# Split of the last phase's down product from chunk 3 instead of 5, and another cut of its first routing

## The reference, cut to what matters

```python
def _L3_ffn_ref(hidden_states, gate_w, gate_bias, w_gate, w_up, w_down, sh_gate, sh_up, sh_down):
    h = hidden_states.reshape(-1, Hd)
    scores = jax.nn.sigmoid(h @ gate_w.T)                    # 32 experts
    sc = scores + gate_bias
    group_scores = jax.lax.top_k(sc.reshape(-1, 8, 4), 2)[0].sum(-1)
    gmask = one_hot(top_k(group_scores, 4)).sum(1)           # 4 of 8 groups
    masked = jnp.where(repeat(gmask, 4) > 0, sc, 0)
    tki = jax.lax.top_k(masked, 8)[1]
    tkw = scores[tki]; tkw = tkw / (tkw.sum(-1) + 1e-20) * 2.5
    combine = (one_hot(tki, 32) * tkw[..., None]).sum(1)
    g = silu(einsum('th,eih->tei', h, w_gate)); u = einsum('th,eih->tei', h, w_up)
    routed = einsum('tei,ehi->th', g * u * combine[:, :, None], w_down)
    shared = silu(h @ sh_gate.T) * (h @ sh_up.T) @ sh_down.T
    return routed + shared
```

## Time and profile before

| | us |
|---|---|
| median of 3 runs | 830.77 |
| lowest, highest | 827.47, 830.89 |
| the profiled execution, its own time | 830.12 |
| its span, first to last instruction | 828.3 |

### The profile page before, as it was taken

One profiled execution on the slowest core, in us unless ns is written; L12 is line 12 of the kernel. 1 busy time (PEld: TensorE's weight loads), 2 busy tenths in 40 slices (PEclk: granted clock), 3 DMA queues, 4 the chain that ended last, 5 costly groups with the idle time before them and its releaser, 6 DMA issues.

```text
span 828.3 us, 13555 instructions
## 1 busy us (share of the span) xinstructions
PE 803.4 (97%) x4387; PEld 558.5 (67%) x4407; DVE 497.6 (60%) x1419; ACT 439.6 (53%) x801; POOL 450.3 (54%) x432
## 2 busy tenths in 40 slices
PE   4999999999999999999999999999999999999998
PEld 4876677676767666665666666656665576677776
DVE  6766536385755637235555767676766647486744
ACT  1434564555646343323667767666566654546543
POOL 5274646557663536467455453454546357575463
PEclk9799999999999999999999999999999999999999
DMA  8213030233414333341233222223122142415151
GB/s 315 81 60 98 6 103 1 64 102 121 144 51 128 77 117 88 114 141 39 64 103 88 79 69 73 72 70 77 36 68 72 33 144 66 152 53 168 56 182 59
DMA packets 44871, 75.29 MB, mean 91 GB/s; under 512 B 8993, under 2 KB 9633, under 8 KB 44673
## 3 DMA queue, kind: packets, MB, share of 16 engines
q1 hardware_dynamic: 44656, 74.42, 30.1%
q10 hardware_dynamic: 144, 0.01, 0.0%
HBM read 56.11 MB, written 1.51 MB: 70 GB/s over the span
## 4 chain that ended last, share of the span: by engine, by line
PE 88%; DVE 7%; ACT 2%; issue 2%; DMA 1%; SPq 0%; DVEq 0%; ACTq 0%
PE Y L979 17%; PE B L892 11%; PE B L894 11%; PE B L893 11%; PE B L1641 5%; PE B L1622 4%; PE B L1660 4%; PE B L1628 3%; PE T L1440 2%; DVE mxh L1931 2%; PE B L1621 1%; PE Y L971 1%; PE Y L970 1%; PE Y L969 1%; PE T L996 1%
## 5 line engine op out<-in xcount | busy, mean ns | idle before, releaser
L1276 POOL TENSOR_TENSOR shared<-shared,bcs 128x512 f32<-128x512 f32 x192 | 247.7, 1296 | 202.7 <-DVE shared L1336 148.9
L1130 ACT ACTIVATE shared<-B 128x512 f32<-128x512 f32 x204 | 121.9, 599 | 206.4 <-PE B L894 205.5
L1336 DVE TENSOR_TENSOR shared<-shared,B 128x512 f32<-128x512 f32 x168 | 114.9, 686 | 172.2 <-PE B L894 132.6
L979 PE MATMUL Y<-shared,down_lo 128*128 128x512 f32 x336 | 172.0, 595 | 0.0
L1870 POOL TENSOR_TENSOR shared_r<-shared_r,const 128x512 fp32r<-128x512 f32 (+1 forms) x128 | 115.7, 936 | 74.3 <-PE B L1622 44.1
L1931 DVE TENSOR_REDUCE mxh<-B 128x4 fp32r<-128x512 f32 (+1 forms) x128 | 78.8, 618 | 81.0 <-PE B L1622 80.0
L1796 ACT ACTIVATE shared<-B 128x512 f32<-128x512 f32 (+1 forms) x128 | 69.5, 543 | 62.5 <-PE B L1628 61.3
L1807 ACT COPY shared<-B 128x512 f32<-128x512 f32 (+1 forms) x128 | 64.5, 504 | 24.8 <-PE B L1641 24.7
L892 PE MATMUL B<-shared_r,gate_hi 128*128 128x512 f32 x102 | 75.0, 736 | 0.0
L1641 PE MATMUL B<-const,shared 128*128 128x128 f32 x448 | 71.5, 276 | 0.7 <-ACT shared L1807 0.7
L892 PE MATMUL B<-x_lo_r,gate_hi 128*128 128x512 f32 x102 | 70.9, 695 | 0.0
(11 more groups left out here) (328 smaller groups left out, 1528.7 us busy)
## 6 DMA issues: line engine op xcount, KB each, us to landing
bcs<-wrow SPq DMA_DIRECT2D x96, 256.0 KB, 3.6
shared_r<-shared_r SPq DMA_DIRECT2D x256, 64.0 KB, 2.0
bcs<-wrow SPq DMA_DIRECT2D x128, 128.0 KB, 3.0
gate_lo<-in_moe SPq DMA_DIRECT2D x9, 256.0 KB, 5.3
up_lo<-in_moe SPq DMA_DIRECT2D x9, 256.0 KB, 6.1
down_lo<-in_moe SPq DMA_DIRECT2D x9, 256.0 KB, 3.7
small<-in_small SPq DMA_DIRECT2D x1, 1372.5 KB, 11.3
X<-in_x SPq DMA_DIRECT2D x4, 256.0 KB, 5.4
```

Source lines behind the costliest of these rows:

```text
L979: nc.tensor.matmul(Y[:], w_raw[2][:, at:at + P], hid[(n0 + c) % HIDDEN], start=(i == 0), stop=(i == m["NC"] - 1))\
L1130: nc.scalar.activation(sg[(n0 + n) % ACTIVE], B[n % GATES][:], ACT.Silu).then_inc(sem("sg_ready"), 1)
L1276: gp.tensor_tensor(by_weight, by_weight, bcs[(PLACE.k0[p] + r // m["PER"]) % BROADCAST], ALU.mult)\
L1336: nc.vector.tensor_tensor(hid[(n0 + n) % HIDDEN], sg[(n0 + n) % ACTIVE], up[:], ALU.mult)\
```

## The change

The routing of phase 7's group 0 is cut in other places: a `yield` behind the reciprocal makes two pieces of the first, and the one behind the groups' mask (`gm`) is left out, so that the mask and the masked scores are one piece. WHOLE goes from 5 to 3: chunks 3 and 4 of groups 1 to 3 are split as well. The high and low parts of the down weights' piece 0 (chunks 3 and 4) are made too, at steps 9 (ScalarE) and 14 (GpSimd); piece 1 moves from step 9 to 10 on ScalarE. `down_hi` takes 14 chunks of columns instead of 12, so `hid_hi` starts one tile higher.

```diff
-        WHOLE, HIGHS = 5, 10
+        WHOLE, HIGHS = 3, 10
...
-        hid_hi = [late.at_tile(18 + i, [P, TG], shared_r) for i in range(HIGHS)]
+        hid_hi = [late.at_tile(19 + i, [P, TG], shared_r) for i in range(HIGHS)]
...
-            return slice((a - WHOLE) * P, (b - WHOLE) * P)
+            return slice((max(a, WHOLE) - WHOLE) * P, (b - WHOLE) * P)
+
+        def down_raw(q):
+
+            a, b = PIECES[7][q]
+            return slice(max(a, WHOLE) * P, b * P)
...
                 st.add(v.reciprocal(t["sig"][:], t["sig"][:]))
                 st.settle()
+                yield
...
             st.add(v.tensor_scalar(t["gm"][:], t["gwork"][:, :, 0:NGR], TAKEN, None, ALU.is_equal))
             st.settle()
-            yield
+            if (p, g) != (7, 0):
+                yield
...
-                    if (g, i) == (1, a):
-                        pe.wait_ge(sem("down_lo_ready"), q)
+                    if (g, i) == (1, max(a, WHOLE)):
+                        pe.wait_ge(sem("down_lo_ready"), q + 1)
...
-        DOWN_ACT = {9: 1, 11: 2, 13: 3}
-        DOWN_POOL = {18: 1, 22: 2, 26: 3}
+        DOWN_ACT = {9: 0, 10: 1, 11: 2, 13: 3}
+        DOWN_POOL = {14: 0, 18: 1, 22: 2, 26: 3}
```

More of the change, by code:

```diff
@@ L1137, in stream_act @@
                     act.wait_ge(sem(f"raw1_{q}"), 96)
-                    nc.scalar.copy(down_hi[:, down_piece(q)], w_raw[2][:, piece(7, q)])\
+                    nc.scalar.copy(down_hi[:, down_piece(q)], w_raw[2][:, down_raw(q)])\
                         .then_inc(sem("down_hi_ready"), 1)
@@ L1280, in stream_pool @@
                     q = DOWN_POOL[n]
-                    c = piece(7, q)
-                    pool.wait_ge(sem("down_hi_ready"), q)
+                    c = down_raw(q)
+                    pool.wait_ge(sem("down_hi_ready"), q + 1)
                     after_down(pool, 7, 0, PIECES[7][q][1] - 1)
```

## The result

The changed kernel takes 832.11 us as the median of 12 runs (829.21 to 833.18); the kernel before, run beside it on the same chip, 829.64 us (12 runs, 827.30 to 830.89). The ratio is 1.0036 with a 95% interval of [1.0025, 1.0046], so the change costs about 3.0 us [2.1, 3.8]; the two medians lie 2.5 us apart. That lies within the 0.5% that the prediction calls the same, and the time lies in its range. But a change of nothing lies outside the interval, and so does the forecast of +0.6 us: the cost is about five times as large.

The account below looks back on a forecast made before the run. TensorE, busy nearly all the time, was taken as the bound. Attention -0.26, group 2's wait +1.5 and later split products -0.64 gave +0.6 us; 830.7 profiled or 831.4 by median, forecast 831.0 us, range 827.7 to 833.2.

Parts of the forecast that it names:

- Part 4: Phase 7, group 2: late weights delay silu 6, so chunk 8's gate product waits, 1.5 us later; group 3 costs nothing.
- bounds of nothing and 2.0 us: Limits on TensorE's shift at group 2's wait: nothing if weights land earlier, 2.0 us if each hop takes 0.1 more.
- Part 1: Attention: cutting the routing's first piece moves unit 6's shift from 649.93 to 648.7; 0.94 us gain after unit 7.
- signs of being wrong: No TensorE idle in group 2, idle in group 1 or 3, or a span moved by more than 3 us.
- rival of a second wait: Group 2's backlog makes TensorE wait for a low part once more, up to 2.0 us: 832.7 us; chance 0.15.
- last rival: Attention stall reappears a unit later, group 1 banks come at VectorE's pace; 830.1 to 830.8 us; chance 0.08.
- Part 3: Phase 7: six down products change from whole to split, 0.16 us each, 0.96 us less TensorE work.
- Part 2: Attention: merged mask and masked scores meet GpSimd, taking back 0.68 us, leaving 0.26; doubted that the pairs would wait.

Follow-up runs that it names:

- e3: Changed kernel with the old routing cuts and chunks 3 and 4 split in group 3 only; 828.77 us, 0.9995 of the kernel before.
- e4: Changed kernel with ScalarE's copy of the turned weights one step earlier, ahead of the cast of chunk 14; 828.76 us, 0.9999 of the kernel before.
- e6: Kernel before with the new routing cuts, GpSimd's last key copy held until VectorE's maximum of unit 7; 828.03 us, 0.9985 of the kernel before.
- e8: e7 with the down product split from chunk 1 on (WHOLE = 1); 827.50 us, 0.9986 of the kernel before.
- e2: Changed kernel with the old routing cuts, so the split from chunk 3 alone; 831.40 us, 1.0030 of the kernel before.
- e7: Changed kernel with the earlier weights copy of e4 and the held key copy of e6; 827.35 us, 0.9977 of the kernel before.
- e1: Kernel before with the new routing cuts alone, split still from chunk 5; 829.69 us, 1.0012 of the kernel before.
- e5: Kernel before with the earlier weights copy of e4, split from chunk 5, old routing cuts; 829.42 us, 0.9999 of the kernel before.

## Why the prediction was right and wrong

**Right: the wait of group 2.** Part 4 named the place, the chain and the order, and each link is in the trace. GpSimd started chunk 3 a little earlier than the chain had it (product at 754.53 + 0.89 = 755.42 in before's time, forecast 755.7), so the table load came 2.47 us later than in the earlier trace rows instead of 2.7. The gate product came 1.22 us later and the one behind it 1.57, where I had 1.5; the idle time itself was 1.17 us, below the 1.5 to 1.8 that I had named. The bounds of nothing and 2.0 us hold both.

**Right: the form of the result.** 42 split down products stand in the trace, six more than before. The unit-6 idle is gone, its shift coming at 647.65 + 1.05 = 648.70 as Part 1 had it, and the kernel is slower by less than 0.5%. The new wait stands at unit 7, but with 1.25 us, where I had some tenths. And one of my own signs of being wrong came: idle time in group 3.

**Wrong: "In group 3 no sigmoid follows, the weighing of chunk 4 at 792.39 waited only for the product, and all of it has 2 us of room. I cost both at nothing."** This is the step that failed, and the largest. The rows told how chunk 4 stood with the weights landing when they did before. But that landing is set by ScalarE's copy at the end of group 2, and Part 4 itself made ScalarE 2.7 us late in group 2. The copy came 3.2 us later against the phase, chunk 3 was weighed 0.9 us late for the DMA alone, and group 3 lost 0.73 us at the wait of 0.47 and 1.08 at the wait of 0.81. At the down product of 795.80, ahead of both waits, TensorE was 0.34 + 0.89 = 1.23 us late against the phase's start, and behind them, at the transposes of group 2's result, 2.19 + 0.89 = 3.08 us: 1.85 us more, in a group where I had counted a gain. I followed the backlog to the next wait and stopped. e3 (no wait in group 3 without group 2's backlog) and e4 (no wait anywhere once the weights land early) show the way it took.

**The rival of a second wait had the size and not the mechanism.** It asked for 2 us through VectorE's backlog and the four upper banks in group 2, with the routing's pieces hitting GpSimd. One such hit is in the trace (1.26 us at 772.88), and it made the backlog longer; but no upper bank was waited for in group 2. The second wait came one group later through the weights. My argument against it, that "the backlog shrinks with every chunk", set the chain's pace (1.95 us a chunk) against TensorE's (2.10). The copy, though, hangs on the chain, and the chain was as late at chunk 10 as at chunk 6 (2.46 us).

**The last rival was half right.** It said that the attention's stall would reappear a unit later through sum and pairs: it did. It also said that TensorE would be handed its banks at VectorE's pace in group 1: what Part 3 saves there is partly lost for this reason, as told below. It didn't have the waits of groups 2 and 3.

**Wrong: Part 2's doubt about the pairs.** I took 0.26 us of gain for the attention and gave 0.8 us of loss as the bound if sum and pairs had to wait for GpSimd's four operations. The attention lost 0.16 us. The pairs rose from 0.52 to 1.70 us beside the key copy and are 0.53 in e6, where the copy is held back. The Trainium skill (SBUF — State Buffer, "Who interferes with whom") says that a VectorE instruction with two SBUF inputs contends with a GpSimd one that reads SBUF, and that the one that issues later is blocked for the whole instruction. The trace agrees: the three pairs took 1.70 us beside GpSimd operations of 0.58 us each, and the masked scores 1.30 us beside one of 1.26 us. That the pairs were short in the earlier trace rows said nothing, because nothing ran on GpSimd beside them there. The loss stayed below the bound because the sum (0.28 us) slipped in ahead. The mask hardly waited (0.23 us at 652.48, 0.18 in phase 7), and the masked scores did (1.30 us, 0.70 in phase 7), but no shift waited for them: with unit 7 already late, TensorE came later.

**Part 3's saving is there, though not all of it.** Once the waits are gone, e4's phase 7 is 0.69 us shorter than before where six times 0.16 is 0.96; in e3 two chunks gave 0.18 of 0.32, in e8 six more gave 0.43 of 0.96. Read against before, e4's TensorE gains 0.30 us at the two chunks of group 1, 0.31 in group 2 and 0.29 in group 3, close to 0.32 each. It loses 0.13 us again late in group 1, most of it at one upper product that starts right behind a low part of VectorE. TensorE and VectorE, e4:

```profile
738.07 0.48 PE L899 MATMUL B<-shared_r,up_hi 128*128 128x512 f32 x1
```

```profile
737.31 0.69 DVE L1324 TENSOR_TENSOR shared_r<-B,shared_r 128x512 fp32r<-128x512 f32 x1
```

The low part ends at 738.00. Before, 0.27 us lay between its end and the upper product, so TensorE can hardly get further ahead there than that. In e8 the wait of 0.16 us stands at the same place. Another 0.08 us goes near the end of group 3, in e3 too; where it goes stays open.

**The sum, put right**: attention +0.16 us (forecast -0.26); behind group 2's wait +1.57 (+1.5); the two split chunks of group 2 -0.34 (-0.32); group 3's two waits +1.85 (nothing); the split chunks of group 3 -0.29 (-0.32). That is 2.95 us, where I had +0.6. The waits of group 3 make 1.85 us of the miss of 2.35, the attention 0.42.

## What to carry to other kernels

When a change makes an engine late, follow the lateness past the first wait: to whatever that engine hands over at the end of the group (here the copy that starts the next group's DMA), and ask what now depends on its landing. A form of work that is cheaper on the busiest engine but needs its input earlier is worth its saving only where that input is early; moving one copy on another engine turned +2.8 us into -0.7 us in that phase. Before a short VectorE operation is moved, look at what GpSimd does at the new place: there, three pairs went from 0.52 to 1.70 us and one of 128 x 4 numbers from 0.17 to 1.26.

## What the runs showed of the hardware

**A 128 x 4 operation can take 1.26 us.** The `tot` row above writes and reads four numbers per partition. It began 0.05 us behind a GpSimd operation of 1.29 us and ended with it. e2, e4, e7 and e8 have the same coincidence and 1.26 to 1.28 us; where the operation falls between two weighings, in before, e1, e3, e5 and e6, it takes 0.17 us. So in these rows the time is set by the neighbour on GpSimd and not by the operation's own size.

**The clock dips behind an idle time in some executions only.** TensorE works at its full clock of 2.4 GHz in this stretch before. The profiled execution of e1 shows, a few microseconds behind the idle time of 1.24 us, a stretch at the lower level of 1.2 GHz (windows: stretch, us, busy time of PE, PEld, DVE, ACT, POOL, granted clock, DMA share, GB/s; a window that holds both levels shows their mean):

```profile
656.00:660.00 4.00, 4.00 (x27) 1.85 (x25) 2.05 (x15) 2.00 (x4) 0.05 (x1) 0.73 0.00 0
```

and e4, where the same work stands:

```profile
656.00:660.00 4.00, 3.91 (x21) 2.45 (x21) 1.12 (x4) 1.40 (x5) 0.00 (x0) 0.62 0.00 0
```

e3 has it too (0.63 in the same window), with the old cut and an idle time of 1.07 us. Before, after, e2 and e5 have idle times of 1.06 to 1.25 us and no dip; e6 to e8, whose longest idle time there is 0.66 us, have none either. It costs 1.4 to 1.6 us of the attention's end (37.10 us in the table beside 35.70 with the old cut, 37.25 and 37.44 beside 35.86 with the new one). So it belongs neither to the cut nor to the split. Nor is this the only place: e1 and e6 have another such stretch between 455 and 465 us, far ahead of anything that the change touches. It follows an idle time of 1.62 us that the kernel before has as well, without a dip. TensorE and the window, e6:

```profile
456.06 0.39 PE L1623 MATMUL B<-maskb,constb 128*128 128x512 bf16 x1 [1.62 <-ACT shared L1798]
```

```profile
455.00:460.00 5.00, 3.94 (x26) 2.86 (x27) 2.83 (x13) 2.65 (x5) 0.39 (x1) 0.79 0.58 182
```

Before, the same idle time ends at 458.41 and the granted clock of 455 to 465 us is 1.00.

Whether a shorter idle time at the attention's end avoids the dip there is not shown. The medians of e6 and e7 gained 0.8 us more than their traces (1.2 against 0.4; 1.9 against 1.1), but e8's did not (1.2 against 1.55), and the intervals hold all of these numbers.

**The start scatters in steps.** The profiled executions differ in how long TensorE stays at the lower clock level near the start of the kernel: 10.2 us before, after, in e1 and e7, 6.8 us in e2 to e4, 3.4 us in e5, e6 and e8. Granted clock from 20 to 30 us, before:

```profile
20.00:30.00 10.00, 9.03 (x44) 8.79 (x43) 7.22 (x31) 3.77 (x8) 2.88 (x2) 0.53 0.30 110
```

and e8:

```profile
20.00:30.00 10.00, 9.03 (x54) 8.24 (x52) 8.36 (x35) 4.79 (x9) 2.87 (x2) 0.83 0.25 91
```

Up to unit 0 of the attention's last cycle all ten kernels do the same work. It is reached at 636.5 to 639.0 us in the four executions with 10.2 us at the lower level, at 635.5 to 635.8 us in the three with 6.8, and at 634.5 us in e5 and e8 with 3.4; e6 (636.65) and e1 (639.0) have the dip at 455 us besides. Runs of one kernel lie 3 to 7 us apart, and these single executions suggest that part of it is decided in this stretch. That is why lengths between two rows of the same execution told 0.2 us here, while the medians tell about one.
